# V of all heads in one pass ahead of the attention, kept in HBM in two parts

## The reference, cut to what matters

```python
sa, ca, ga, sb, cb, gb = mod                       # (silu(c) @ W_mod), six parts
h = layernorm(x) * (1 + ca) + sa                   # x: 2048 x 512
k, q, v = W_K h, W_Q h, W_V h                      # 16 heads of 128
scores = k . q ; masked = causal(scores)
attn = softmax(masked / sqrt(512))
z = attn @ v
x = x + ga * (W_O z)
h = layernorm(x) * (1 + cb) + sb
x = x + gb * rmsnorm(W_down (silu(W_gate h) * W_up h))
```

## Time and profile before

| | |
|---|---|
| median of 3 runs | 2183.33 us (2177.83 to 2184.59) |
| the profiled execution's own time | 2183.67 us |
| its span, first to last instruction | 2181.7 us |
| PE busy | 2112.4 us, 97% of the span |
| DVE, ACT, POOL busy | 1353.7, 1059.6, 719.3 us |
| moved by DMA | 122.79 MB, 56 GB/s over the span |

### The profile page before, as it was taken

The page is one execution under the profiler, slowest core; times in us unless marked ns, Lnnn a source line. Parts: engine busy times, 40 slices in busy tenths (PEclk is TensorE's granted clock), DMA queues, the critical chain, the costliest instruction groups (busy, mean ns, idle before and its releaser), DMA issues. The chain is left out here.

```text
span 2181.7 us, 37262 instructions
## 1 busy us (share of the span) xinstructions
PE 2112.4 (97%) x12305; PEld 1845.1 (85%) x12305; DVE 1353.7 (62%) x3062; ACT 1059.6 (49%) x2006; POOL 719.3 (33%) x546
## 2 busy tenths in 40 slices
PE   6899999999999999999999999999997999899899
PEld 3698989898889989898988989898986788788687
DVE  7465655656565656556565646455564587699865
ACT  4354545455454545445454545455453333588511
POOL 3333343334243343443350101000017344388300
PEclk9999999999999999999999999999998999999999
DMA  5111110110111010111100000000006576111121
GB/s 207 40 41 35 35 34 32 35 43 22 46 46 34 34 34 31 34 34 34 46 25 26 25 12 24 12 22 15 25 21 192 175 245 221 57 40 39 46 70 63
DMA packets 84004, 122.79 MB, mean 56 GB/s; under 512 B 9315, under 2 KB 49891, under 8 KB 83939
## 3 DMA queue, kind: packets, MB, share of 16 engines
q1 hardware_dynamic: 81635, 117.76, 16.6%
q10 hardware_dynamic: 2304, 4.20, 0.5%
HBM read 87.97 MB, written 33.95 MB: 56 GB/s over the span
## 5 line engine op out<-in xcount | busy, mean ns | idle before, releaser
L978 DVE TENSOR_TENSOR pT_lo<-ps_t,pT_hi 128x512 fp32r<-128x512 f32 (+3 forms) x640 | 360.3, 605 | 219.9 <-ACT pT_hi L895 219.7
L903 ACT ACTIVATE probs<-probs,rmin 128x128 f32<-128x128 f32 (+15 forms) x256 | 307.9, 1203 | 225.7 <-DVE rmin L969 224.7
L895 ACT ACTIVATE pT_hi<-ps_t 128x512 fp32r<-128x512 f32 (+3 forms) x640 | 304.9, 534 | 87.5 <-PE ps_t L831 86.2
L197 PE MATMUL ps_z<-pT_hi,v_hi 128*128 128x256 f32 (+1 forms) x1152 | 326.4, 283 | 0.0
L198 PE MATMUL ps_z<-pT_lo,v_hi 128*128 128x256 f32 (+1 forms) x1152 | 325.4, 282 | 0.0
L199 PE MATMUL ps_z<-pT_hi,v_lo 128*128 128x256 f32 (+1 forms) x1152 | 324.8, 282 | 0.0
L197 PE MATMUL ps_p<-hT_hi,w_hi 128*128 128x512 f32 x768 | 309.6, 403 | 8.6 <-PEq L277 4.1
L199 PE MATMUL ps_p<-hT_hi,w_lo 128*128 128x512 f32 x768 | 301.9, 393 | 0.0
L198 PE MATMUL ps_p<-hT_lo,w_hi 128*128 128x512 f32 x768 | 301.2, 392 | 0.0
L831 PE MATMUL ps_t<-ident,probs 128*128 128x128 f32 x2176 | 278.9, 274 | 3.1 <-DVE pT_lo L978 1.6
L831 PEld LDWEIGHTS ps_t<-ident,probs 128*128 128x128 f32 x2176 | 247.3, 141 | 19.1 <-DVE pT_lo L978 2.1
(11 more groups left out here) (140 smaller groups left out, 3861.2 us busy)
## 6 DMA issues: line engine op xcount, KB each, us to landing
scratch_zT<-z SPq DMA_DIRECT2D x256, 64.0 KB, 1.6
o_z<-scratch_zT SPq DMA_DIRECT2D x31, 512.0 KB, 7.0
o_scales<-scratch_recips SPq DMA_DIRECT2D x31, 512.0 KB, 7.8
w_raw<-in_w_qkv SPq DMA_DIRECT2D x16, 768.0 KB, 4.6
p_wmod<-in_w_mod SPq DMA_DIRECT2D x6, 1024.0 KB, 10.6
words<-in_gu_packed SPq DMA_DIRECT2D x44, 128.0 KB, 3.5
scratch_wgu<-deq_a SPq DMA_DIRECT2D x22, 256.0 KB, 2.0
g_codes<-scratch_wgu SPq DMA_DIRECT2D x11, 512.0 KB, 3.4
```

The costliest lines, as they stand in the source:

```text
L197: nc.tensor.matmul(dst, stat[0], mov[0], start=start, stop=False)
L895: nc.scalar.activation(pT[0][:, slot, i % 2, 0:w], ps_t[:, (chunks_before(i) + u) % T_BANKS, 0:w], ACT.Copy).then_inc(t_hi, 1)
L903: nc.scalar.activation(probs[:, i % 2, 0:w], probs[:, i % 2, 0:w], ACT.Exp, bias=rmin[:, i % 2:i % 2 + 1], scale=-1.0, accum_out=sums[:, i ...
L978: nc.vector.tensor_tensor(pT[1][:, slot, i % 2, 0:w], ps_t[:, (chunks_before(i) + u) % T_BANKS, 0:w], pT[0][:, slot, i % 2, 0:w].bitcast(F ...
```

## The change

V leaves the attention. The prologue makes V of all heads: for a tile of 128 tokens and a group of four heads (`values`), hT is the stationary side and the weights of four heads, 512 columns, the moving side. The result stands with tokens on partitions at once. There are 4 groups of heads by 16 token tiles, so 64 units `V0` to `V63` of 12 matmuls each, into two PSUM banks `p_psv`. ACT makes the high part and DVE the low part in two buffers `p_vo`, and SP stores both (256 KB each) in HBM. W_V is loaded four heads at a time and split (ACT and POOL for the first group, POOL alone after that). The first 16 units are interleaved with the rest of the prologue's work by five new written orders, one for each engine; the others follow.

In the attention, the unit PV, the transposes PW and the copies UV and UW are gone. Each head loads its V from HBM in four quarters of two transfers (`load_v`), quarter u as soon as the previous head's last pair has read it (`z_read_v`). The written orders of PE, ACT and DVE are new ones. Q and K keep their units; the first three units of the coming head are made at a head's end as before, now Q0, K0, K1 in place of Q0, K0, V0.

```diff
-UNITS = [("Q", 0), ("K", 0), ("V", 0), ("VT", 0)] + [(kind, b) for b in range(1, NB) for kind in ("K", "Q", "V", "VT")]
+UNITS = [("Q", 0), ("K", 0)] + [(kind, b) for b in range(1, NB) for kind in ("K", "Q")]
...
+    PE_FIRST = """M0 M1 T0.0 T0.1 T0.2 T0.3 T1.0 T1.1 V0 V1 M2 T1.2 T1.3 V2 V3 T2.0 V4 T2.1 T2.2 T2.3 V5 V6 V7 V8 V9
+        V10 T3.0 T3.1 T3.2 V11 T3.3 M3 V12 V13 V14 M4 M5 V15"""
+    DVE_FIRST = """S0 G0 N0 G1 S1 L0.0 L0.1 L0.2 N1 L0.3 S2 S3 X0 L1.0 X1 G2 N2 X2 X3 L2.0 X4 N3 X5 X6 X7 X8 X9 X10 L3.0
+        X11 G3 X12 X13 X14 G4 G5 X15"""
+    POOL_FIRST = """I0 I1 I2 I3 WK WQ L1.1 J1.0 J1.1 L1.2 L1.3 J1.2 J1.3 L2.1 L2.2 L2.3 L3.1 L3.2 L3.3"""
+    SP_FIRST = """Rc Rm0 Rx0 Rm1 Rv0 Rx1 Rx2 Rx3 Rw Rm2 Rm3 Rv1 O0 O1 Rm4 O2 O3 O4 Rv2 O5 O6 O7 O8 O9 O10 O11 Rm5 O12
+        O13 O14 O15"""
...
+        def save_v(n):
+            g, t = divmod(n, NT)
+            sp.wait_ge(v_lo, n + 1)
+            for k in range(2):
+                sp.dma_start(hbm["v"][k, t, :, g * HG:(g + 1) * HG, :], vo[k][:, n % 2, :, :].bitcast(F32)) \
+                  .then_inc(v_saved[n % 2], 16)
...
+        def value_hi(n):
+            act.wait_ge(v_ready, n + 1)
+            if n >= 2:
+                act.wait_ge(v_saved[n % 2], 2 * 16 * (n // 2))
+            nc.scalar.activation(vo[0][:, n % 2, :, :].rearrange("p h n -> p (h n)"), ps_v[:, n % 2, :], ACT.Copy) \
+              .then_inc(v_hi, 1)
...
+        def value_lo(n):
+            dve.wait_ge(v_hi, n + 1)
+            nc.vector.tensor_tensor(vo[1][:, n % 2, :, :].rearrange("p h n -> p (h n)"), ps_v[:, n % 2, :],
+                                    vo[0][:, n % 2, :, :].rearrange("p h n -> p (h n)").bitcast(F32),
+                                    ALU.subtract).then_inc(v_lo, 1)
...
+        def values(n):
+
+            g, t = divmod(n, NT)
+            if t == 0:
+                pe.wait_ge(wv_lo, HG * (g + 1))
+            if n >= 2:
+                pe.wait_ge(v_lo, n - 1)
...
+                ht = [part[:, c, t * P:(t + 1) * P] for part in (hT_hi, hT_lo)]
+                w = [part[:, g % 2, :, c * DH:(c + 1) * DH] for part in wv]
+                last = split_matmul(nc, dst, ht, w, c == 0, c == DC - 1)
+            last.then_inc(v_ready, 1)
...
+        def load_v(h, u):
+
+            if not is_at(h, 0):
+                if u < NB - 1:
+                    sp.wait_ge(z_read_v, (NB - 1) * (h - 1) + u + 1)
+                else:
+                    sp.wait_ge(z_ready, NPAIR * h)
+            for k in range(2):
+                sp.dma_start(v[k][:, u * TPB:(u + 1) * TPB, :].bitcast(F32),
+                             hbm["v"][k, u * TPB:(u + 1) * TPB, :, bass.ds(h, 1), :].rearrange("t p a n -> p t (a n)")) \
+                  .then_inc(v_loaded[u], 16)
...
-            pe.wait_ge(proj_lo, lo_count(h, ("VT", u)))
+            if b == 2 * u:
+                pe.wait_ge(v_loaded[u], 2 * 16 * (h + 1))
```

More of the change, by code:

```diff
@@ L350, in prologue @@
-    lo_odd = sem("p_lo_odd")
-    idx_step = sem("p_idx_step")
+    ps_t = ph.enter_context(nc.psum_tensor("p_pst", [P, DC, BT], F32))
+    ps_v = ph.enter_context(nc.psum_tensor("p_psv", [P, 2, BT], F32))
+    c_loaded = sem("c_loaded")
+    x_loaded = [sem(f"x_loaded{b}") for b in range(NB)]
+    wm_loaded = [sem(f"wm_loaded{s}") for s in range(SECTIONS)]
+    wv_loaded = sem("wv_loaded")
+    const_zeroed = sem("const_zeroed")
+    const_ready = sem("const_ready")
+    c_ready = sem("c_ready")
@@ new lines, in save_v @@
+        def save_v(n):
[4 more added lines that the diff above has]
+                  .then_inc(v_saved[n % 2], 16)
+        for what, arg in entries(SP_FIRST):
+            if what == "R":
+                load(arg)
+            else:
+                save_v(int(arg))
+        for n in range(V_FIRST, NV):
+            if n == V_FIRST + 6:
+                load("v3")
+            save_v(n)
@@ L384, in _ @@
+        for n in range(2):
+            sp.wait_ge(v_saved[n], 2 * 16 * NV // 2)
     @block.gpsimd
@@ new lines, in wv_high @@
+        def wv_high(a):
+            if a == 0:
+                act.wait_ge(wv_loaded, 16)
+            nc.scalar.activation(wv[0][:, 0, a, :], wv_raw[:, a, :], ACT.Copy).then_inc(wv_hi, 1)
+        def value_hi(n):
[4 more added lines that the diff above has]
+              .then_inc(v_hi, 1)
+        for what, arg in entries(ACT_FIRST):
+            {"D": deviation, "H": wv_high, "A": modulate, "Y": value_hi}[what](*numbers(arg))
@@ L584, in attention @@
     z_ready = sem("z_ready")
+    z_read_v = sem("z_read_v")
+    v_loaded = [sem(f"v_loaded{n}") for n in range(NB)]
     z_copied = sem("z_copied")
@@ L663, in head @@
         def head(h, decode, first, last):
+            for u in range(NB if first else 2):
+                load_v(h, u)
             if last:
-                sp.wait_ge(w_split, 6 * H)
+                sp.wait_ge(w_split, SPLITS * H)
                 for n in range(3):
@@ L675, in head @@
                 save_z(h - 1, NPAIR - 2)
+                for u in range(2, NB):
+                    load_v(h, u)
                 save_last_z(h - 1)
@@ L848, in pv @@
                     last = split_matmul(nc, ps_z[:, 0:2 * P], vv, p, k == 0, False)
+                    if b == NPAIR - 1 and k == TPB * u + TPB - 1:
+                        last.then_inc(z_read_v, 1)
                 else:
@@ L879, in unit_hi @@
             act.wait_ge(proj_ready, NU * h + UNIT_AT[(kind, b)] + 1)
[L880 to L885 removed]
+            if kind == "Q":
                 ins = nc.scalar.activation(qT[0][:, b % 2, :], ps_p[:, :], ACT.Copy, scale=-SOFT)
@@ L937, in unit_lo @@
             dve.wait_ge(proj_hi, NU * h + UNIT_AT[(kind, b)] + 1)
-            if kind == "VT":
-                parts = [part[:, b * TPB:(b + 1) * TPB, :].rearrange("p t n -> p (t n)") for part in v]
-            elif kind == "Q":
+            if kind == "Q":
                 parts = [part[:, b % 2, :] for part in qT]
```

346 lines of the change are left out of this document (179 added, 167 removed).

## The result

The changed kernel takes 2281.02 us (median of 4, 2277.55 to 2285.29) against 2182.05 us (median of 4): the ratio is 1.0456, 95% interval 1.043 to 1.0483. It is 99 us slower where 30 us faster was forecast. The profiled execution has a span of 2275.8 us.

A forecast was written before the change was run, and what follows sets the result against it. PE was taken to bound the kernel: 28 us of transposes removed, some 4 us of idle prologue filled, a little lost at the ends, giving 2153.5 us, 30 below the profiled 2183.67; range 2146 to 2172.

The forecast's parts named there:

- Does PE go on without waiting?: Attention: PE work between the tightest pairs covers their chains; no added wait in repeated heads, up to 1 us a head for range.
- a wait there holds only transfers that have tens of us: SP's queue in the attention: V's loads stand ahead of the weights' load and z's saves, which were said to have time.
- The removal: Attention: V's projection (175.1 us) and transposes (27.9) leave PE, 203.0 us, 12.7 a head; a head should take 86.8 us.
- the three chains: Attention: scores to transposes (4.7 us cover against 3.7), transposes to product (2.1 against 1.5), PK1 to PQ1 (2.5 against 1.7).
- V's loads: Attention: each quarter's two transfers take 4 us where 9.5 us of PE work lie between; hidden, price 0.
- The pass keeps PE's pace: Prologue: a buffer round of 4.6 us fits in two units' 5.48 us, so PE sets the pace, 2.74 us a unit.
- Rival 3: Prologue's pass: stores set the pace if a pair takes over 4.0 us, 31 us per us above; about 2250 at 7.2; chance 0.09.
- Rival 1: Attention: PE starts to wait in heads; 2169 at 1 us a head, no gain at 1.9; 0.27 shared with Rival 2.
- Rival 2: Prologue hides nothing: attention starts at 233.6 to 240 us, time 2158 to 2165; chance 0.27 shared with Rival 1.
- V0's start: Prologue: first V unit on PE taken at 27 us, after loads, statistics and normalising that end at 26 to 29.
- the later waits: Prologue after the first V unit: 1 us for block 2's slow normalising plus a half-clock stretch, together 3 us.
- the last part ahead of the attention: Prologue's end: last unit's copies, two stores and the engines' meeting, 4.9 us in place of 4.07; attention starts at 228.8.

The follow-up runs named there:

- three_buffers: Changed kernel, written orders kept, with separate words and codes buffers for each of three pieces, all loaded ahead of V's loads: 2171.4 us, ratio 0.9952.
- x_late: Changed kernel with the three unpackings of 4-bit words moved later in DVE's written order: 2179.06 us, ratio 0.9984 to the kernel before.
- x_later: Changed kernel with the three unpackings moved later in DVE's order, the third to behind C12.1: 2158.12 us, ratio 0.9894 to the kernel before.
- before_x_close: Kernel before, V still made in the attention, with the three unpackings put closer together in DVE's order: 2227.54 us, ratio 1.0208.
- three_buffers_pool: three_buffers with POOL's prologue order changed, the split of K's and Q's weights moved to the end: 2166.98 us, ratio 0.9927.

## Why the prediction was wrong

**The step that failed** is "Does PE go on without waiting?", and with it the sentence on SP, "a wait there holds only transfers that have tens of us". I measured the distance between PE's own words, and only for the chains of scores and transposes. There the added wait was put at nothing in the repeated heads; measured it is 12 us in each head that decodes. The words that DVE executes for another job, the unpacking, were not looked at: they stand in the same ordered list, they wait for SP, POOL and a transfer, and the new order had moved them. The trace of before had what was needed. The unpackings were 22.3 and 20.3 us apart, and POOL waited for them 412.6 us in all, so they ran with slack. Unpacking, decoding, issue and transfer make a floor of 16.1 us for the distance. In the new order DVE comes to X1 11.6 us after X0 and to X2 12.6 us after X1, where nothing makes it wait (three_buffers). x_late, x_later and before_x_close move only the places of the three words and take the loss away or bring it; three_buffers removes the floor and takes it away too.

**The sum, against the trace.** The attention was forecast to end at 1634.5 us and ends at 1763.1. The difference of 128.6 is: 10.0 of later start, 116.6 in the ten heads that decode (984.6 less 868), and 2.0 for the first and the last heads together. What follows took 4.3 us less than before. Of the 116.6 us in the ten heads, 76.1 are PE's idle time (984.58 less 908.48), and the granted clock of 0.97 makes some 30 more; about 1 us a head is not accounted for. The heads differ in it. In the head shown, PE is idle for 6.6 us and a stretch at the half clock follows each wait; in the one from 747.74 to 845.45 us it is idle for 8.3 us at a granted clock of 0.98. So PE's idle times of 2 to 3 us are sometimes followed by the half clock and sometimes not, in before_x_close in three of ten heads.

**What held.** The removal is worth 12.7 us a head (86.77 us in heads 11 to 13, and 87.3 in x_later's heads that decode). The margins of 0.5 to 1 us of the three chains were enough. V's loads come in time. The pass keeps PE's pace at 2.75 us a unit; the pair of stores lands in 2.6 and 3.3 us, near the 3.1 that was worked out. **Rival 3** is thus out: ACT does wait for stores, 50 us in all, but PE loses some 1.3 us, once, 10 us after a load of W_V was issued. The Trainium skill's 2 us for HBM at high load (DMA: Bandwidth & Descriptors, Latency and other measured facts) does not show here with writes at 193 GB/s: the two stores of 256 KB landed 0.6 and 1.3 us later than the 2.0 us of the earlier trace rows.

**The rivals.** **Rival 1** named the right place, waits in the heads, but gave it the wrong mechanism and too small a price, up to 1.9 us a head. **Rival 2** came true in part: the attention starts 10 us late. Mis-sized there were V0's start (27, measured 31.2) and the later waits (3 us, measured 8: the pass takes 202.0 us, to 233.18, where the work is 193.9), both with normalising that takes 5.1 us twice where I had let it go up to 4.5, and the last part ahead of the attention (4.9, measured 5.6). That is 4.2, 5.1 and 0.7, the 10.0 us.

**Luck in the repaired kernel.** A time that included these would be 2163.5. x_later, with the waits for words gone, is at 2158.1, inside the forecast's range, but in part by luck: its attention ends 13.1 us later than forecast (1647.6 against 1634.5), and what follows takes 508.9 us in place of 517.0, 6.1 of it in the output projection, where the granted clock is 0.99 and in the kernel before 0.96.

## What to carry to other kernels

When a hand-written order is shortened, check every job that rides in it, the side jobs first: for each resource that goes round several engines and a transfer, compare the length of the round with the distance of its uses in the new order. An engine at 60% busy can still stop the one at 100%, if it executes in order and one of its instructions waits for a transfer. And heads, tiles or iterations of two kinds in one trace are a free experiment: here the heads without decoding showed at once that the forecast of the removal was right and where the loss was.

## What was unexpected of the hardware

- DVE's normalising of a block (four instructions, one SBUF tensor in and out) takes 1.9 us beside an idle POOL and 5.1 beside a working one, on the same data shapes. In three_buffers and three_buffers_pool, which differ in POOL's order alone, the same instructions are:

```profile
24.48 5.07 DVE L563 TENSOR_SCALAR p_xn<-p_x,p_mv,p_rstd 128x512 f32<-128x512 f32 x4
...
24.66 1.92 DVE L563 TENSOR_SCALAR p_xn<-p_x,p_mv,p_rstd 128x512 f32<-128x512 f32 x4
```

  The Trainium skill (SBUF — State Buffer, SBUF: two separate sides) describes a port pair of the two engines that is an exclusive lock held for a whole instruction. The trace fits it: beside the working POOL each of the four takes 1.1 to 1.5 us in place of 0.55, about as long as the POOL instruction next to it (1.0 to 1.3 us).
- What a wait of DVE costs PE is not its length. In the changed kernel a head's 10.1 us cost 12.4, at a granted clock of 0.95; in x_late a wait of 3.1 us cost 2.0, at 1.00 (88.80 against 86.77 us).
